# A decoder layer on one core: in the steps that hold an output projection, the next input's first half is transposed ahead of that projection

## The reference

```python
x = layernorm(x + self_attention(x, wq, wk, wv, wo))            # 16 query heads, 8 key/value heads, rotary, causal
x = layernorm(x + cross_attention(x, ctx, Wq, Wkv_expand, Wout))  # 16 heads of 32, causal mask: only the first 512 context rows count
x = layernorm(x + ffn(x, w1, w2, w3))                          # silu(x w1) * (x w2), then w3; weights through an NF4 round trip
```

## Time and profile before

| What | Value |
|---|---|
| median of 3 runs | 1108.55 us (1103.7 to 1111.01) |
| the profiled execution's own time | 1107.93 us |
| its span in the profile | 1106.2 us |
| PE busy (matmul) | 1027.2 us, 93% |
| DVE busy | 754.4 us, 68% |
| ACT busy | 481.8 us, 44% |
| POOL busy | 432.7 us, 39% |

### The profile page before, as it was taken

The page is one execution under the profiler, slowest core; times in us unless marked ns, Lnnn a source line. Parts: engine busy times, 40 slices in busy tenths (PEclk is TensorE's granted clock), DMA queues, the critical chain, the costliest instruction groups (busy, mean ns, idle before and its releaser), DMA issues.

```text
span 1106.2 us, 17645 instructions
## 1 busy us (share of the span) xinstructions
PE 1027.2 (93%) x6280; PEld 664.9 (60%) x6280; DVE 754.4 (68%) x1684; ACT 481.8 (44%) x587; POOL 432.7 (39%) x462
## 2 busy tenths in 40 slices
PE   8999999999999899998979989998999999999995
PEld 7454555555455454565546556554657888888884
DVE  7888658657866589558776876886675645463635
ACT  3434344644465465546764664675451212111110
POOL 3558566976687564123252323333266100000000
PEclk9999899999999999999999999999999999999998
DMA  6832576386636773746765575757536203011021
GB/s 233 228 98 38 135 194 188 92 238 186 182 100 166 197 211 100 175 90 150 205 160 125 125 201 120 167 136 178 128 74 229 91 1 114 1 40 37 1 76 39
DMA packets 92618, 145.17 MB, mean 131 GB/s; under 512 B 22506, under 2 KB 39794, under 8 KB 92274
## 3 DMA queue, kind: packets, MB, share of 16 engines
q1 hardware_dynamic: 83218, 116.49, 40.4%
q0 software_dynamic: 8000, 26.75, 8.7%
q10 hardware_dynamic: 1312, 0.79, 0.2%
HBM read 78.09 MB, written 23.73 MB: 92 GB/s over the span
## 4 chain that ended last, share of the span: by engine, by line
PE 62%; DVE 16%; DMA 6%; issue 5%; ACT 5%; POOL 4%; SPq 2%; ACTq 1%; DVEq 0%; POOLq 0%
PE att_pv L1040 10%; PE att_pv L1293 7%; PE att_scores L1293 7%; PE att_scores_T L1323 7%; PE att_scores_T L1013 6%; PE att_scores L979 5%; PE att_scores_T L965 5%; PE att_scores_T L967 5%; PE att_scores_T L966 5%; DVE att_mx L1657 3%; DVE att_scores L1651 2%; PE att_scores_T L1158 2%; DMA att_nf_home<-nf_reciprocals 2%; DVE att_nf_zone L1811 2%; ACT att_probs L1460 1%
## 5 line engine op out<-in xcount | busy, mean ns | idle before, releaser
L1460 ACT ACTIVATE att_probs<-att_scores_T 128x1024 f32<-128x1024 f32 (+2 forms) x256 | 217.5, 884 | 146.6 <-PE att_scores_T L1013 144.1
L1040 PE MATMUL att_pv<-att_probs,att_v 128*32 128x512 f32 (+3 forms) x1024 | 210.4, 525 | 0.8 <-POOL att_probs L842 0.6
L1040 PE MATMUL att_pv<-att_probs,att_ones 128*32 128x512 f32 (+3 forms) x1024 | 210.3, 526 | 0.0
L1657 DVE TENSOR_REDUCE att_mx<-att_scores 128x1 f32<-128x512 f32 x248 | 159.0, 682 | 73.4 <-PE att_scores L979 71.7
L979 PE MATMUL att_scores<-att_k_stack,att_q_stack 96*128 96x256 f32 (+1 forms) x504 | 171.2, 402 | 15.2 <-DVE att_mx L1657 7.1
L1013 PE MATMUL att_scores_T<-att_q_stack,att_k_stack 97*128 97x512 f32 (+2 forms) x512 | 139.5, 383 | 9.8 <-ACT att_raw L1398 2.4
L1651 DVE CUSTOM_DVE_ANT_0 att_scores<-att_scores,att_cmask 128x128 f32<-128x128 f32 (+3 forms) x256 | 120.9, 511 | 37.7 <-PE att_scores L979 36.1
L842 POOL TENSOR_SCALAR_AFFINE_SELECT att_probs<-att_probs 128x256 f32<-128x256 f32 x128 | 57.4, 448 | 192.8 <-ACT att_probs L1460 189.9
L979 PEld LDWEIGHTS att_scores<-att_k_stack,att_q_stack 96*128 96x128 f32 x504 | 88.4, 190 | 63.1 <-DVE att_mx L1657 24.3
L1013 PEld LDWEIGHTS att_scores_T<-att_q_stack,att_k_stack 97*128 97x128 f32 x512 | 85.7, 189 | 51.7 <-issue 19.4
L1550 ACT ACTIVATE att_probs<-att_scores 128x512 f32<-128x512 f32 x44 | 26.3, 598 | 207.4 <-PE att_scores L1293 207.4
(11 more groups left out here) (262 smaller groups left out, 2091.5 us busy)
## 6 DMA issues: line engine op xcount, KB each, us to landing
att_q_stack<-att_q_hi SPq DMA_DIRECT2D x128, 128.0 KB, 3.2
att_probs<-nf_x SPq DMA_DIRECT2D x28, 352.0 KB, 3.7
att_nf_home<-nf_reciprocals POOLq DMA_DIRECT2D x48, 176.0 KB, 4.9
att_q_stack<-att_q_lo SPq DMA_DIRECT2D x64, 128.0 KB, 3.6
att_k_stack<-att_k_hi SPq DMA_DIRECT2D x64, 128.0 KB, 3.4
att_nf_home<-nf_x SPq DMA_DIRECT2D x20, 352.0 KB, 3.8
w_nf<-att_nf_zone SPq DMA_DIRECT2D x192, 22.0 KB, 2.5
att_k_stack<-att_k_hi SPq DMA_DIRECT2D x64, 64.0 KB, 4.3
```

The lines of the kernel that those rows point to most:

```text
L1040: last = T.matmul(pv[HD * j:HD * j + HD, sums, q0:S], lhs, pr[:, at:at + S - q0], start=(t == 0), stop=(t == TT - 1))
L1460: A.activation(probs_of(b, r)[:, 1024 * h:1024 * h + w], bank[:, 0:w], ACT.Exp, scale=SCALE).then_inc(st_free, 1)
L1657: V.tensor_reduce(mx[:, p % 2, TT * r + t:TT * r + t + 1], sco[:, r, :], AX.X, ALU.max).then_inc(sc_free, 1)
```

## The change

In every step (b, 1) whose next input is crossed (b = 3 to 7; b = 1 and 2 make nothing of the next input in their step 1 and aren't crossed, so they stay as they are):

- The ring's order becomes exp 2, exp 3, x0, out 0, round mid, out 1, round end.
- PE transposes x0 ahead of out 0 instead of behind out 1. For a crossed b (4 to 7) PE also issues maxima 2 ahead of x0 instead of between out 0 and the mid rounding; for b = 3 it stays there.
- ACT evacuates x0 right behind exp 3 (and the passes that stand there), ahead of the end rounding's passes and, in b = 3, ahead of the two weight copies of that step.
- DVE takes maxima 2 ahead of the mid passes (crossed b), and cuts x0 behind the mid passes and ahead of `add_residual` 0, where it was the last thing of the step.

No instruction is added or removed.

```diff
--- before.py
+++ after.py
@@ -183,11 +183,13 @@
             order += [("exp", b, p, 2), ("exp", b, p, 3)]
             mid, end = rounds_of(b, p)
             if p == 1 and b > 0:
+                order += [("raw", b + 1, what) for what in made(b + 1, p)]
                 order.append(("out", b - 1, 0))
                 if mid is not None:
                     order.append(("round", mid))
                 order.append(("out", b - 1, 1))
-            order += [("raw", b + 1, what) for what in made(b + 1, p)]
+            else:
+                order += [("raw", b + 1, what) for what in made(b + 1, p)]
             if (b, p) == (0, 4):
                 order += [("sums",), ("rec",)]
             if (b, p) == (1, 0):
@@ -1227,13 +1229,16 @@
                     if ahead:
                         weigh(b, p, 0)
                     if p == 1 and b > 0:
+                        if crossed(b):
+                            maxima(*fore, 2)
+                        for half in range(2):
+                            make(b + 1, whats, half)
                         project_out(b - 1, 0)
-                        maxima(*fore, 2)
+                        if not crossed(b):
+                            maxima(*fore, 2)
                         if mid is not None:
                             rounding(mid)
                         project_out(b - 1, 1)
-                        for half in range(2):
-                            make(b + 1, whats, half)
                         maxima(*fore, 3)
                     elif crossed(b) and whats:
 
@@ -1514,6 +1519,9 @@
                     exponential(b, p, 3)
                     if mid is None and 0 in mine and behind:
                         exceed(end, 0)
+                    if p == 1 and b > 0:
+                        for what in made(b + 1, p):
+                            evacuate(b + 1, what)
                     if (b, p) == (B - 1, 1):
                         act.wait_ge(wq_in, 32)
                         for h, src in enumerate((rsw, rsum)):
@@ -1531,7 +1539,7 @@
                         for h in range(2):
                             k = slice(2 * h, 2 * h + 2)
                             hi_of_weights(wh[:, k, 1024:1536], y[:, k, :])
-                    for what in made(b + 1, p):
+                    for what in made(b + 1, p) if p != 1 else ():
                         evacuate(b + 1, what)
                     if (b, p) == (0, 4):
                         copy_scalers(("sums",), sumf, NW)
@@ -1858,9 +1866,14 @@
 
                         maxima(*fore, 0)
                         maxima(*fore, 1)
+                        if crossed(b):
+                            maxima(*fore, 2)
                         exceeds(mid, range(4))
+                        for what in made(b + 1, p):
+                            cut_raw(b + 1, what)
                         add_residual(b - 1, 0)
-                        maxima(*fore, 2)
+                        if not crossed(b):
+                            maxima(*fore, 2)
                         if mid is not None:
                             scale_rounded(mid)
                         moments(b - 1, 0)
@@ -1872,8 +1885,6 @@
                         moments(b - 1, 1)
                         if not late(b):
                             begin_spread(range(TT))
-                        for what in made(b + 1, p):
-                            cut_raw(b + 1, what)
                         continue
                     if fore:
                         maxima(*fore, 0)
```

## The result

Four runs of the changed kernel: median 1118.61 us (1117.86 to 1119.69), beside 1108.0 us for the kernel before; ratio 1.0085, 95% interval 1.0053 to 1.0116. Eleven more runs on another occasion gave 1.0068 (1.0041 to 1.0095). So it is 7.5 to 9.4 us slower. That is under 1%, but both intervals exclude no change, and the first median lies 6.7 us over the predicted 1111.9. It is also 0.1 us over the predicted range's end of 1118.5; the ratio 1.0085 on the 1108.55 us that the prediction started from gives 1118.0, and the second measurement's median, 1116.16 us, lies inside. All ratios leave out three runs that took over 1.5% longer than the fastest of their kernel: 1122.56 and 1832.82 us with x0 early in b = 4 to 7, 1610.23 us with exp 3 first in b = 4. The profiled execution took 1117.87 us, span 1116.0, which is 9.8 us more than the span before.

The account below looks back on a forecast made before the run. PE, busy 93% of the span, bounds the kernel, so only its gaps count. Steps b = 3 to 7 sum 0.5 + 1.39 + 0.28 + 1.36 - 0.2 = +3.3 us on 1108.55: 1111.9 us, range 1105 to 1118.5 us.

Parts of the forecast that it names:

- Out 0 waits for exp 3: Steps (b, 1), b = 3 to 7: out 0 waits for exp 3 instead of exp 2; 3.06 us later in b = 6.
- b = 5: Step (5, 1): out 0 starts at 585.75 in place of 583.77; 1.98 - 1.70 = +0.28 us.
- b = 6: Step (6, 1): out 0 starts 3.06 us later, less 0.79 and 0.91 us given back; +1.36 us.
- The 0.91 us go: PE's wait ahead of maxima 1 in step (b, 2) goes, since DVE cuts x0 earlier; -0.91 us per crossed step.
- those 1.01 us as they are: The wait ahead of the rounding at the end of (b, 2), behind DVE's threshold pass, stays at 1.01 us.
- its move is worth nothing: In steps with a mid rounding, moving maxima 2 ahead gains nothing; out 1 still starts 1.61 us behind out 0's end.
- D: Rival: PE's 0.91 us wait stays, DVE's chain being held by something else; +0.9 us in four steps, 1115.5 us; chance 0.08.
- C: Rival: the 1.01 us ahead of (b, 2)'s rounding go too in b = 4, 5, 6; +0.3 us, 1108.9 us; chance 0.14.
- B: Rival: out 0 hardly waits for exp 3, starting when x0 is done; -4.1 us, 1104.4 us; chance 0.08.
- B = 4: 3.09 us: Step (4, 1): out 0 starts at 486.78 in place of 483.69, 3.09 us later; step cost +1.39 us.
- The rest costs nothing: ACT's x0 copies, POOL's load of x1 (issued some 13 us sooner) and SP's loads add no cost; b = 3 totals +0.5 us.
- Rival A: The clock falls in one or both of b = 4 and 6; 3.4 us each, 1115.3 or 1118.7 us; chance 0.28.

Follow-up runs that it names:

- exp 3 first in b = 4: The changed kernel, with ACT doing exp 3 ahead of the mid rounding's threshold pass in b = 4 alone; ratio 1.0012 to the kernel before.
- the late cut: The changed kernel, with DVE's cut of x0 back at the step's end in b = 4 to 7; ratio 1.0092 to the kernel before.
- maxima back: The changed kernel, with maxima 2 back between out 0 and the mid rounding on PE and DVE; ratio 1.0083 to the kernel before.
- the kernel with POOL held: The changed kernel, with POOL's load of x1 in b = 3 held until out 1 has left PE; ratio 1.0066 to the kernel before.
- x0 early in b = 4 to 7 with maxima 2 back: The changed kernel with b = 3 in old order, exp 3 ahead of ACT's threshold pass in b = 4 to 7, maxima 2 behind out 0; ratio 0.9970 to kernel before.

## Why the prediction was partly right

- **"Out 0 waits for exp 3", "b = 5", "b = 6", "b = 7":** right: the wait, its cause and its size, and each step's cost within 0.5 us. But b = 5 to 7 hold only 0.3 of the 9.6 us that the table adds up to. That the loss stayed under 1% (11 us) was close, with a forecast sum of 3.3 us, and is partly luck.
- **"The 0.91 us go", "those 1.01 us as they are", "its move is worth nothing":** right in the traces; the late cut brings the 0.91 us back, and maxima back brings no gain. D and C fall. So does B.
- **"B = 4: 3.09 us":** mis-sized. It took 4.43 us (2.78 to 3.36 us of it wait). I took the rows' landing, 3.8 us behind the issue, from one execution. Over the fourteen profiled executions, that load in (4, 1) took 3.8 us in four and 4.5 to 5.2 in ten, also in kernels where x0 isn't early there (5.0 and 4.9). Before, its lateness hid behind out 0; the change put it on the path. Where the load took 3.8 us with out 0 waiting for exp 3 behind the pass, in the late cut's profile, out 0 waited 1.98 us, near the 2.3 forecast. What makes it late stays open.
- **"The rest costs nothing", for b = 3:** this step failed. I looked at where x1's load lands, not at what stands behind it on POOL. The divide came 1.45 us earlier and met DVE's passes, which took 2.59 us in place of 1.29, and PE waited 1.64 us. Predicted +0.5 us; this execution +5.3, 3.4 of it clock; x0 early in b = 3 alone 3.3 us over its runs (0 to 6.6).
- **Rival A, "price 3.4 us each":** the clock did fall behind b = 4's wait, costing 1.7 us in the first profile, and with it behind b = 3's, which I hadn't named; behind b = 6's not in that profile. I had given it 0.28. Its 1118.7 us is near the measured time, but by other places and other terms: that the numbers meet is luck.
- **The baseline:** the profile of before is the only one of the fourteen with no clock loss between 200 and 1088 us; the others lost 1.7 to 13.7 us there (windows of 8 us). Its mean clock was 0.990; the mean over 34 runs of the same kernel is 0.984. My sum took its rows for the usual case.

## What to carry to other kernels

When a unit moves up in a ring, every unit behind it waits for another reader: look at what stands between the two readers on their engine, and move the reader up with it. A load that nobody waited for has a scatter that one profile doesn't show; ask what its slow end costs before putting it on the path. On a queue that loses a wait, follow the instruction behind the one that waited, to the engine that it then runs beside.

## What the runs showed of the hardware

**DVE's bf16 passes and POOL's operations hold each other up.** In the fourteen profiles a pass of 128 x 1408 takes 0.58 us (median; 0.57 to 0.77) while POOL computes nothing. Of the 109 passes that began while a POOL TENSOR_TENSOR ran, 102 ended 0.38 to 0.40 us behind it: DVE at 395.54, POOL at 395.16. Of those that began up to 0.8 us ahead of one, some were stopped the same way (397.57 against 397.58: DVE's end 399.51, POOL's 399.11), and some not: in the kernel with POOL held a pass at 428.76 took 0.57 us, and POOL's divide, begun 0.05 us behind it, took 1.91 us in place of 1.53. DVE's cut of x0 (two inputs in SBUF, 1.23 us) took 2.10 and 2.56 us beside POOL's TENSOR_TENSORs. DVE's maxima, f32 from PSUM, take 0.68 us in the median beside POOL and without it. Passes were held up in the old order too. The kernel of x0 early in b = 4 to 7 with maxima 2 back has b = 3 as before:

```profile
390.25 3.93 DVE L1829 TENSOR_SCALAR att_nf_zone<-att_nf_home,att_nf_limits 128x1408 bf16<-128x1408 bf16 x2 [0.61 <-DMA att_nf_home<-nf_x]
394.29 2.29 DVE L1829 TENSOR_SCALAR att_nf_home<-att_nf_home,att_nf_limits 128x1408 bf16<-128x1408 bf16 x1
...
390.88 2.41 POOL L820 TENSOR_TENSOR att_w_lo<-att_turned,att_w_hi 128x1024 fp32r<-128x1024 f32 x1
...
394.64 1.54 POOL L768 TENSOR_TENSOR att_nf_home<-att_nf_home 128x704 bf16<-128x704 bf16 x1
```

Its rows came early, the passes ran into POOL's weight subtraction, and the end rounding waited 2.80 us. The Trainium skill, "SBUF — State Buffer", says in "SBUF: two separate sides" that the port pair that DVE and GpSimd share is a lock that whichever starts first holds for its whole instruction, so that the other stands still. The trace agrees that one of the two stands still, in either direction (1.94 us for a pass, 1.91 for a divide); who wins can't be told from the profile's start times (397.57 lost to 397.58).

**Where the clock falls.** In the six profiles with a wait of 1.98 to 3.36 us ahead of b = 4's out 0, with x0's transposes ahead of it, the clock fell there in all six; in the eight without such a wait, in none. Ahead of b = 3's end rounding, waits of 1.64 to 2.80 us were followed by a fall in all seven profiles that had one, shorter or no waits in none of seven. But the 2.6 us ahead of b = 4's last rounding (2.57 us ahead of 566.89 in the kernel before, clock 1.00 behind it) was followed by a fall in three of ten. Nor need there be a long wait: in b = 5, with x0 waiting 0.50 us and out 0 0.75, the clock held in the first profile of the changed kernel (1.00 in the 4 us from out 0's start) and fell in that of the late cut (0.57). The length of a wait doesn't decide by itself. The Trainium skill, "TensorE: Matmul & The Clock Gate", "Part 4: PE-mode transpose", says that the full clock doesn't engage for transposes, which don't count as PE-busy in the same way. That fits b = 4, but no run here had such a wait without them; at b = 6, with 1.86 to 1.99 us and the same transposes, it fell in two of four. What decides was not tried.
